# Key sums beside the value blocks, two last quotients in free banks, counts by column block, transfers in two parts and a layer norm in column chunks

## The chip, the core and the metric

The kernel runs on one core of one Trainium2 chip. Its engines run side by side and wait for one another through semaphores: TensorE (PE, with its weight loads PEld), VectorE (DVE), ScalarE (ACT), GpSimd (POOL) and SyncE (SP), which mostly issues transfers to the 16 DMA engines. The metric is the device time of one execution in microseconds; a few executions are timed and their median is compared. One execution is taken by the profiler.

## What is computed

A network of two layers on 1250 nodes of 768 features and 20000 edges. Cut to what matters here:

```
xn = layernorm(x)
x  = x + gcn(xn, edges) + linear_attention(xn)     # layer 0
x  = x + top2_of_8_experts(layernorm(x))
xn = layernorm(x)
x  = x + gat(gat(xn, 4 heads of 512), 1 head of 768) + flow_attention(xn)   # layer 1
x  = x + top2_of_16_experts(layernorm(x)) + shared_expert(layernorm(x))

layernorm(x) = (x - mean(x)) / sqrt(var(x) + 1e-5)
linear_attention: q, k = elu(.) + 1;  out = (q (k^T v)) / (q sum(k))   per head of 64
gat: e = leaky_relu(al_s[src] + al_d[dst]); softmax of e over the edges into a node; sum of h[src] by it
```

The edges are turned once into a dense matrix of counts (1250 by 1250); the graph parts multiply with it.

## The kernel before

The program is a list of stages, each a block in which every engine has its own code; a barrier ends each block. Nodes are laid out in two ways: node-major, ten tiles of 125 nodes on 125 partitions (`NT = 125`, `TILES = 10`), and feature-major, six tiles of 128 features on 128 partitions with 1254 columns, that is three chunks of `CW = 418` (`CH = 3`), which fill a bank of the 8-bank PSUM tensor `ps` each. Products that must be exact are made of three passes of rounded halves; others are plain float32 matmuls, which stand in the trace as two records each.

The stages that the change touches, in order of time:

- `norm_nodes_stage` loads the features x node-major in two transfers of five tiles (L139), takes statistics (L149), scales and transposes.
- `linear_attention_stage` makes keys and values for all ten tiles in `la_kv`, then for each of six blocks of 128 features (two heads) the product of keys and values (L258, ten tiles, bank p) and, into two more columns of the same bank, the product of the keys with a tile of ones (L261): the key sums. VectorE masks both into `kvb` and `denb`. Then q is projected, three chunks per block, and each of 18 units (block and chunk) gets a numerator (L270, bank 6) and a denominator (L271, bank 7); VectorE takes the reciprocal (L372) and multiplies (L374) before the next unit may write the two banks. TensorE runs four units behind the projection, so the last four follow it alone.
- `counts_stage` builds the counts row tile by row tile and stores for each a tile `far` (L437, 125 partitions, two buffers) that marks the absent edges; the stage ends when the last is stored (L439).
- `aggregate_stage` casts the counts to int16, tile by tile (L604), stores them to `counts_keep` (L617) and multiplies with them on TensorE (L673).
- `norm_stage`, three times (`ln1`, `ln2`, `ln3`): on feature-major x, TensorE averages all six tiles over 1254 columns (L806), VectorE subtracts (L818), ScalarE squares (L835), TensorE averages the squares (L811), then eps (L822), root (L837), reciprocal (L824) and scaling (L827), each over all 1254 columns.
- `graph_project_stage` projects to the four heads, tile by tile; ScalarE copies each result out of PSUM (L1946) and issues its store to `h_projected` itself (L1948, 40 of 250 KB). Far rows come in on SP (L1847).
- `graph_heads_stage`: per head and chunk the weights p of ten tiles are made (L2166, exponential, then times the counts in L2174), GpSimd sums them, TensorE aggregates the head's features with them (L2075). SP issues, in this order, the counts in three parts by tiles (L2051), the first head's features (L2043, 2500 KB on 125 partitions), the bias (L2053) and the second head's features.
- `graph_layer`, once, with one head: logits, then ten maxima over far rows (L2489, loaded by L2284 into two buffers), then weights and aggregation as above.

Transfers that SP issues go to its queue in the order of the code.

## Time and profile before

| | |
|---|---|
| median of 3 runs | 3528.55 us (3520.45 to 3528.65) |
| profiled execution, its own time | 3522.21 us |
| span of the profiled execution | 3520.4 us |
| PE busy | 2805.8 us (80%) |
| DVE busy | 1561.8 us (44%) |
| ACT busy | 829.2 us (24%) |
| moved by DMA | 314.17 MB, mean 89 GB/s |

The span is that of the profiled instructions; the execution's own time has what lies around it. Busy shares are means over stages with different limits, so what a stage waits for is read in that stage. PEclk in the windows is the granted TensorE clock, 1.00 for 2.4 GHz and 0.50 for 1.2 GHz.

### The profile page before, as it was taken

The page shows a single profiled execution, that of the slowest core. Times are in us where ns is not written, and L with a number is a line of the kernel's source. Part 1 is how long each engine was busy: PE and PEld are TensorE (multiplying, and loading weights), DVE is VectorE, ACT ScalarE, POOL GpSimd, SP SyncE. Part 2 cuts the span into 40 slices and gives each one's busy share as a digit, 9 for nine tenths or more (in the row PEclk, how much of TensorE's full clock was granted, in tenths as well). Part 3 has the DMA queues.
Part 4 walks back from the last instruction along what each step waited for, and adds up shares of the span by engine and source line. Part 5 has one row for each costly group of instructions (what it writes and reads, how often), then busy time and mean ns, then how long its engine had stood idle before and what let it go on. Part 6 is the DMA issues. An engine that isn't in the chain of part 4 may idle for free. (4 is left out here: it accounts for less than half of the span.)

```text
span 3520.4 us, 33065 instructions
## 1 busy us (share of the span) xinstructions
PE 2805.8 (80%) x12434; PEld 2168.8 (62%) x12434; DVE 1561.8 (44%) x2347; ACT 829.2 (24%) x1133; POOL 258.6 (7%) x251
## 2 busy tenths in 40 slices
PE   3997888897289767999999589995963966938884
PEld 3995454595289736857677445553962536727773
DVE  4327884413245434132345178872126433215554
ACT  2100012101145303201222234432102111025551
POOL 0000000000200100000000123320002100020002
PEclk9999999997589868979899799996985986969996
DMA  3500003200388512100223211104211001066664
GB/s 120 215 19 7 8 22 121 98 19 1 90 300 287 173 43 77 32 9 13 71 78 115 85 61 59 59 35 121 62 56 36 0 1 54 1 193 236 231 210 154
DMA packets 110470, 314.17 MB, mean 89 GB/s; under 512 B 40860, under 2 KB 50741, under 8 KB 101156
## 3 DMA queue, kind: packets, MB, share of 16 engines
q1 hardware_dynamic: 70572, 224.26, 18.4%
q10 hardware_dynamic: 21856, 57.43, 4.4%
q0 software_dynamic: 17920, 30.81, 3.3%
q8 instruction: 81, 1.33, 0.2%
q14 instruction: 41, 0.34, 0.0%
HBM read 215.33 MB, written 97.05 MB: 89 GB/s over the span
## 5 line engine op out<-in xcount | busy, mean ns | idle before, releaser
L2075 PE MATMUL ps<-g_p,g_h 125*128 125x418 f32 x960 | 341.9, 516 | 51.4 <-DMA g_h<-h_projected 51.4
L2075 PEld LDWEIGHTS ps<-g_p,g_h 125*128 125x128 f32 x960 | 182.8, 191 | 208.4 <-issue 156.5
L1097 PE MATMUL ps<-e_wh,e_xh 128*128 128x384 f32 (+1 forms) x600 | 220.6, 368 | 0.5 <-DVE e_wl L1316 0.5
L1097 PE MATMUL ps<-e_wh,e_xl 128*128 128x384 f32 (+1 forms) x600 | 214.1, 357 | 0.0
L1097 PE MATMUL ps<-e_wl,e_xh 128*128 128x384 f32 (+1 forms) x600 | 214.0, 357 | 0.0
L1326 DVE TENSOR_TENSOR e_xl<-ps,e_xh 128x768 fp32r<-128x768 f32 x68 | 65.1, 958 | 212.1 <-ACT e_xh L1267 212.1
L1097 PE MATMUL ps<-w_hi,h_hi 128*125 128x384 f32 x320 | 113.7, 355 | 43.2 <-DVE w_lo L2663 43.2
L1194 PE MATMUL ps<-ident,e_x 128*128 128x128 f32 x408 | 58.5, 282 | 111.1 <-DMA e_x<-expert_rows 111.1
L2351 PE MATMUL ps<-g_p,normed 125*128 125x418 f32 x360 | 130.1, 523 | 19.5 <-DVE g_p L2530 19.5
L2166 DVE SCALAR_TENSOR_TENSOR ps<-g_rows,g_logits,normed 125x418 f32<-125x418 f32 x120 | 126.8, 1066 | 34.0 <-DMA g_bias<-in_L_b 16.3
L548 PE MATMUL ps<-hot_src,hot_dst 125*125 125x418 f16 x588 | 125.8, 369 | 3.6 <-DVE hot_dst L492 3.6
L673 PE MATMUL ps<-counts,x 125*128 125x418 f32 x360 | 126.6, 513 | 0.0
L1316 DVE TENSOR_TENSOR e_wl<-e_w,e_wh 128x3072 fp32r<-128x3072 f32 (+1 forms) x34 | 101.4, 2982 | 46.2 <-ACT e_wh L1257 46.2
L2146 POOL TENSOR_TENSOR normed<-normed,g_p 125x418 f32<-125x418 f32 x108 | 109.7, 1016 | 133.7 <-DVE g_p L2174 130.3
L1097 PEld LDWEIGHTS ps<-e_wh,e_xl 128*128 128x128 f32 x600 | 113.6, 189 | 9.2
L1194 PEld LDWEIGHTS ps<-ident,e_x 128*128 128x128 f32 x408 | 49.0, 145 | 113.4 <-DMA e_x<-expert_rows 112.3
L1097 PEld LDWEIGHTS ps<-e_wh,e_xh 128*128 128x128 f32 x600 | 113.7, 190 | 8.1 <-issue 0.8
L1097 PEld LDWEIGHTS ps<-e_wl,e_xh 128*128 128x128 f32 x600 | 113.9, 190 | 7.6
L2351 PEld LDWEIGHTS ps<-g_p,normed 125*128 125x128 f32 x360 | 69.4, 193 | 79.4 <-issue 59.6
L491 DVE TENSOR_SCALAR hot_src<-index_row,edge_float 125x1254 f16<-125x1254 f16 x196 | 106.7, 544 | 25.5 <-PE ps L541 23.7
L1097 PE MATMUL ps<-attT_lo,la_hi 128*125 128x384 f32 x360 | 104.4, 345 | 12.4 <-DVE attT_lo L334 12.3
L1097 PE MATMUL ps<-w_lo,h_hi 128*125 128x384 f32 x320 | 111.7, 349 | 0.0
(433 smaller groups left out, 6058.9 us busy)
## 6 DMA issues: line engine op xcount, KB each, us to landing
e_w<-in_L_experts SPq DMA_DIRECT2D x32, 1152.0 KB, 6.2
e_w<-in_L_experts SPq DMA_DIRECT2D x18, 1536.0 KB, 7.1
e_x<-expert_rows SPq DMA_DIRECT2D x68, 384.0 KB, 5.1
expert_rows<-e_y ACTq DMA_DIRECT2D x68, 384.0 KB, 4.2
expert_rows<-la_zeros ACTq DMA_DIRECT2D x13, 1536.0 KB, 15.4
e_w<-in_L_experts SPq DMA_DIRECT2D x18, 768.0 KB, 5.1
h<-normed SPq DMA_DIRECT2D x48, 209.0 KB, 1.9
h_projected<-gp_h ACTq DMA_DIRECT2D x40, 250.0 KB
```

The costliest lines, as they stand in the source:

```text
L491: nc.vector.tensor_scalar(hs[:, u, :], idx[:], ef[:, 0, bass.ds(e, 1)], None, ALU.is_equal)
L548: mm = nc.tensor.matmul(ps[0:NT, b + c, 0:CW], hd[:, u, :], hs[:, u, cols(c)], start=False, stop=False, skip_group_check=True)
L673: mm = nc.tensor.matmul(ps[:, 3 * (f % 2) + c, 0:CW], k.x_node[:, t, P * f:P * f + P], k.counts[:, t, cols(c)], start=(t == 0), stop=(t == ...
L1097: mm = nc.tensor.matmul(out, lhs[a], rhs[b], start=(start and m == 0), stop=(stop and m == 2))
L1194: mm = nc.tensor.transpose(ps[:, f // 3, P * (f % 3):P * (f % 3) + P], x[:, b.x, P * f:P * f + P], k.ident[:])
L1316: nc.vector.tensor_tensor(wlo[:, b.w, 0:W1], w[:, b.w, 0:W1], whi[:, b.w, 0:W1].bitcast(F32), ALU.subtract)\
L1326: nc.vector.tensor_tensor(xlo[:, b.x, :, :].rearrange("p (b f) n -> p b (f n)", b=2), ps[:, 0:2, 0:3 * P], xhi[:, b.x, :, :].rearrange("p ...
L2075: mm = nc.tensor.matmul(ps[:, f, 0:CW], h_sb[:, i % 2, t, P * f:P * f + P], pr[:, n % 2, t, :], start=(t == 0), stop=(t == TILES - 1))
L2146: nc.gpsimd.tensor_tensor(sm[:, n % 2, :], sm[:, n % 2, :], pr[:, n % 2, t, :], ALU.add)\
L2166: nc.vector.scalar_tensor_tensor(out=t1(m), in0=rows[0:NT, i, 0, cols(c)], scalar=k.al[:, t, i:i + 1], in1=t2[:, m % 2, :], op0=ALU.add, o ...
L2351: mm = nc.tensor.matmul(ps[:, f, 0:CW], h_sb[:, i % HB, t, P * f:P * f + P], pr[:, n % 2, t, :], start=(t == 0), stop=(t == TILES - 1))
```

## The change

- *Key sums*: the value half of `la_kv` gets two columns of ones beside each block of 128 (`VW = 130`), set once by a memset; one product of 130 columns per tile and block gives values and sums. The 60 matmuls with the tile of ones are gone.
- *Last quotients*: `nd_bank` gives units 16 and 17 banks 0, 1 and 2, 3, which the projection no longer needs, and they no longer wait for the quotient before.
- *Counts by column block*: `counts_keep` and its copies are laid out by chunk (125 x 3 x 10 x 418). The head stage loads the first chunk, then the first head's features, then the other chunks; each chunk is waited for at its first use.
- *Transfers in two parts*: `two_parts` issues a transfer over 125 partitions as one of 112 and one of 13, each adding 16 to the semaphore; the waits ask for 32. It is used for the features, far rows (stores and both loads), counts (store and loads), the stores of `h_projected` and its loads.
- *Layer norm in chunks*: means, centring, squares, variances, roots and scaling run by chunk of 418 columns, in a staggered order, in `ln1`, `ln2` and `ln3`.

The diff, cut to its core:

```diff
+def two_parts(eng, dst, src, sem):
+
+    for part in (slice(0, 112), slice(112, NT)):
+        eng.dma_start(dst[part], src[part]).then_inc(sem, 16)
...
-                    sp.dma_start(k.x_node[:, 5 * g:5 * g + 5, :],
-                                 x_dram[625 * g:625 * g + 625, :].rearrange("(t p) d -> p t d", p=NT)).then_inc(loaded[g], 16)
+                    two_parts(sp, k.x_node[:, 5 * g:5 * g + 5, :],
+                              x_dram[625 * g:625 * g + 625, :].rearrange("(t p) d -> p t d", p=NT), loaded[g])
...
+        def nd_bank(v):
+
+            return 6 if v <= UNITS - CH else 2 * (v - UNITS + CH - 1)
...
-                        nc.tensor.matmul(ps[:, p, 0:P], kv[0:NT, t, P * p:P * p + P], kv[0:NT, t, D + P * p:D + P * p + P],
-                                         start=(t == 0), stop=(t == TILES - 1))
-                    for t in range(TILES):
-                        mm = nc.tensor.matmul(ps[:, p, P:P + 2], kv[0:NT, t, P * p:P * p + P], k.ones[0:NT, 0:2],
+                        mm = nc.tensor.matmul(ps[:, p, 0:VW], kv[0:NT, t, P * p:P * p + P], vb[:, t, p, :],
                                               start=(t == 0), stop=(t == TILES - 1))
...
-                    if v >= 1:
-                        pe.wait_ge(s["nd_out"], v)
-                    p, c = v // CH, v % CH
-                    nc.tensor.matmul(ps[:, 6, 0:CW], kvb[:, p, :], q[:, p % 2, cols(c)], start=True, stop=True)
-                    nc.tensor.matmul(ps[:, 7, 0:CW], denb[:, p, :], q[:, p % 2, cols(c)], start=True, stop=True)\
+                    if v <= UNITS - CH:
+                        if v >= 1:
+                            pe.wait_ge(s["nd_out"], v)
+                    p, c, b = v // CH, v % CH, nd_bank(v)
+                    nc.tensor.matmul(ps[:, b, 0:CW], kvb[:, p, :], q[:, p % 2, cols(c)], start=True, stop=True)
+                    nc.tensor.matmul(ps[:, b + 1, 0:CW], denb[:, p, :], q[:, p % 2, cols(c)], start=True, stop=True)\
...
+                nc.vector.memset(vb[:, :, :, P:VW], 1.0).then_inc(s["ones"], 1)
...
-                    nc.scalar.activation(whole[:, t, :], k.counts[:, t, :], ACT.Copy).then_inc(cast, 1)
+                    nc.scalar.activation(whole[:, :, t, :], k.counts[:, t, :].rearrange("p (c n) -> p c n", c=CH), ACT.Copy).then_inc(cast, 1)
...
-                sp.dma_start(k.counts_dram[:, :, :], whole[:]).then_inc(kept, 16)
+                two_parts(sp, k.counts_dram, whole[:], kept)
...
+                means(0)
+                means(1)
+                variances(0)
+                means(2)
+                variances(1)
+                variances(2)
...
+                def scale(c):
+                    dve.wait_ge(root, c + 1)
+                    nc.vector.reciprocal(r[:, c, :], r[:, c, :]).then_inc(rec, 1)
+                    dve.wait_ge(rec, c + 1)
+                    for f in range(FC):
+                        nc.vector.tensor_tensor(k.nT[:, f, cols(c)], k.nT[:, f, cols(c)], r[:, c, :], ALU.mult)
+                centre(0, range(FC))
+                centre(1, range(FC))
+                spread(0)
+                centre(2, range(FC))
+                scale(0)
+                spread(1)
+                spread(2)
+                scale(1)
+                scale(2)
...
+                squares(0)
+                squares(1)
+                roots(0)
+                squares(2)
+                roots(1)
+                roots(2)
...
-                        sp.dma_start(k.far_dram[t], far[:, t % 2, 0:T]).then_inc(far_out[t % 2], 16)
...
-                    act.dma_start(h_dram[n // TILES, :, n % TILES, :], h[:, n % HR, :]).then_inc(st[n % HR], 16)
+                    two_parts(act, h_dram[n // TILES, :, n % TILES, :], h[:, n % HR, :], st[n % HR])
...
-                    sp.dma_start(h_sb[:, i % 2], h_dram[i]).then_inc(h_in[i % 2], 16)
+                    two_parts(sp, h_sb[:, i % 2], h_dram[i], h_in[i % 2])
...
-                for q, (a, b) in enumerate(parts):
-                    sp.dma_start(counts[:, a:b, :], k.counts_dram[:, a:b, :]).then_inc(c_in[q], 16)
+                two_parts(sp, counts[:, 0], k.counts_dram[:, 0], c_in[0])
                 head_in(0)
+                for c in range(1, CH):
+                    two_parts(sp, counts[:, c], k.counts_dram[:, c], c_in[c])
...
-                        sp.dma_start(far[:, n % 2, :], k.far_dram[t]).then_inc(far_in[n % 2], 16)
+                        two_parts(sp, far[:, n % 2, :], k.far_dram[t], far_in[n % 2])
```

On SP, at the start of the graph heads, these transfers stood in the queue before (the counts, the features of the first head, the bias, the features of the second head):

```order
L2051 DMA g1_counts<-counts_keep 125x2508
L2051 DMA g1_counts<-counts_keep 125x5016 x2
L2043 DMA g1_h<-h1_projected 125x5120
L2053 DMA g1_bias<-in_L1_b1 128x16
L2043 DMA g1_h<-h1_projected 125x5120
```

And these stand there now, up to the second chunk of the counts; the third chunk, the bias and the second head follow:

```order
L98 DMA g1_counts<-counts_keep 112x4180
L98 DMA g1_counts<-counts_keep 13x4180
L98 DMA g1_h<-h1_projected 112x5120
L98 DMA g1_h<-h1_projected 13x5120
L98 DMA g1_counts<-counts_keep 112x4180
L98 DMA g1_counts<-counts_keep 13x4180
```

The first head's features moved ahead of two thirds of the counts, and ahead of the bias stand now eight issues instead of four.

On DVE, in the layer norm `ln1` (`normed` is the result, `ln_r` the root and its inverse), from the end of the projection before to the start of the router behind, this stood before:

```order
L787 SCALAR_TENSOR_TENSOR x<-ps,x_bias,x 128x1254 x2
L700 UNCONDITIONAL_BRANCH
L814 UNCONDITIONAL_BRANCH
L818 TENSOR_TENSOR normed<-x,ps 128x1254 x6
L822 TENSOR_SCALAR ln_r<-ps 128x1254
L824 RECIPROCAL ln_r<-ln_r 128x1254
L827 TENSOR_TENSOR normed<-normed,ln_r 128x1254 x6
L801 UNCONDITIONAL_BRANCH
```

And this stands there now:

```order
L841 TENSOR_TENSOR normed<-x,ps 128x418 x12
L845 TENSOR_SCALAR ln_r<-ps 128x418
L841 TENSOR_TENSOR normed<-x,ps 128x418 x6
L849 RECIPROCAL ln_r<-ln_r 128x418
L852 TENSOR_TENSOR normed<-normed,ln_r 128x418 x6
L845 TENSOR_SCALAR ln_r<-ps 128x418 x2
L849 RECIPROCAL ln_r<-ln_r 128x418
L852 TENSOR_TENSOR normed<-normed,ln_r 128x418 x6
```

The centring of the third chunk moved behind the first chunk's eps addition, and the first chunk's reciprocal and scaling ahead of the other two eps additions; the third chunk's reciprocal and scaling end the list.

## Rows read from the trace of the kernel before

**Rows 1.** The head of the page.

```profile
span 3520.4 us, 33065 instructions
```

**Rows 2.** Windows: length, busy time of PE, PEld, DVE, ACT, POOL, PEclk, DMA share, GB/s.

```profile
19.40:34.40 15.00, 0.00 (x0) 0.00 (x0) 4.70 (x10) 0.00 (x0) 0.00 (x0) 1.00 0.31 122
```

**Rows 3.** Timeline at the start: start us, duration us, engine, line, operation.

```profile
1.88 5.79 SPq L139 DMA_DIRECT2D x<-in_x  x2
34.46 4.70 DVE L149 BATCH_NORM_STATS2 ln_six<-x 125x6 f32<-125x384 f32 x10 [10.33 <-DMA x<-in_x]
```

**Rows 4.** DMA issues: tiles, queue, count, KB each, median us to landing.

```profile
x<-in_xT SPq DMA_DIRECT2D x1, 3750.0 KB, 13.6
fa_w<-in_L_v SPq DMA_DIRECT2D x6, 384.0 KB, 3.1
```

**Rows 5.** Timeline of the key and value products, first and last block.

```profile
196.60 2.39 PE L258 MATMUL ps<-la_kv 125*128 125x128 f32 x20
225.41 4.27 PE L261 MATMUL ps<-ones,la_kv 125*128 125x2 f32 x20
```

**Rows 6.** Windows, columns as in rows 2: the last block of sums.

```profile
226.00:230.00 4.00, 4.00 (x19) 4.00 (x19) 0.28 (x3) 0.00 (x0) 0.00 (x0) 0.50 0.00 0
```

**Rows 7.** Timeline of the last quotients.

```profile
339.20 2.77 DVE L372 RECIPROCAL la_kv<-ps 128x418 f32<-128x418 f32 x1 [3.31 <-PE ps L271]
342.74 1.69 PE L270 MATMUL ps<-la_kv,la_w 128*128 128x418 f32 x2 [3.58 <-DVE attT L374]
345.87 2.77 DVE L372 RECIPROCAL la_kv<-ps 128x418 f32<-128x418 f32 x1 [3.27 <-PE ps L271]
```

**Rows 8.** Timeline of the first layer norm of this form.

```profile
814.97 12.89 PE L806 MATMUL ps<-x,avg 128*128 128x418 f32 x36 [1.95 <-PEq L700]
830.70 14.61 PE L811 MATMUL ps<-ln_sq,avg 128*128 128x418 f32 x36 [2.84 <-ACT ln_sq L835]
848.12 7.99 DVE L824 RECIPROCAL ln_r<-ln_r 128x1254 f32<-128x1254 f32 x1 [1.31 <-ACT ln_r L837]
856.14 8.34 DVE L827 TENSOR_TENSOR normed<-normed,ln_r 128x1254 f32<-128x1254 f32 x6
```

**Rows 9.** Timeline: the second norm's means, the third one's variances.

```profile
1294.68 14.79 PE L806 MATMUL ps<-x,avg 128*128 128x418 f32 x36 [12.58 <-PEq L79]
2859.01 15.98 PE L811 MATMUL ps<-ln_sq,avg 128*128 128x418 f32 x36 [2.84 <-ACT ln_sq L835]
```

**Rows 10.** Groups by line: count, busy us, mean ns of one, idle before.

```profile
L374 DVE TENSOR_TENSOR attT<-ps,la_kv 128x418 f32<-128x418 f32 x18 | 10.7, 594 | 0.6
L835 ACT ACTIVATE ln_sq<-normed 128x1254 f32<-128x1254 f32 x18 | 22.5, 1249 | 261.3 <-DVE normed L818 246.2 <-PE ps L811 14.7
```

**Rows 11.** Waits of the SP queue: us in total, times, longest.

```profile
SPq L439 <- DMA far<-far_rows: 4.5, 1, 4.5
```

**Rows 12.** Timeline at the start of the graph heads.

```profile
1987.80 1.02 SPq L2051 DMA_DIRECT2D g_counts<-counts_keep  x3
1995.66 0.59 DVE L2174 SCALAR_TENSOR_TENSOR g_p<-ps,g_counts 125x418 f32<-125x418 f32 x1 [3.36 <-DMA g_counts<-counts_keep]
2007.03 0.58 DVE L2174 SCALAR_TENSOR_TENSOR g_p<-ps,g_counts 125x418 f32<-125x418 f32 x1
2009.13 0.58 DVE L2174 SCALAR_TENSOR_TENSOR g_p<-ps,g_counts 125x418 f32<-125x418 f32 x1
2034.19 9.77 PE L2075 MATMUL ps<-g_p,g_h 125*128 125x418 f32 x20 [51.44 <-DMA g_h<-h_projected]
```

**Rows 13.** Waits of the compute engines: us in total, times, longest.

```profile
ACT gp_h L1946 <- PE ps L1097: 99.8, 31, 7.2
DVE g_diag L2489 <- DMA g_far<-far: 15.1, 8, 3.2
```

**Rows 14.** Timeline of the maxima in the last graph layer.

```profile
2651.56 1.46 DVE L2489 CUSTOM_DVE_ANT_0 g_diag<-g_rows,g_far 125x1250 bf16<-125x1250 f32 x1 [3.16 <-DMA g_far<-far]
```

**Rows 15.** Timeline of ScalarE in the projection, its longest issue.

```profile
1865.64 1.19 ACTq L1948 DMA_DIRECT2D h_projected<-gp_h  x1
```

More of the change, by code:

```diff
@@ L254, in _ @@
                         mm.then_inc(s["kv_done"], 1)
+                pe.wait_ge(s["ones"], 1)
                 for p in range(FC):
@@ L814, in _, with variances @@
+                def variances(c):
+                    for f in range(FC):
+                        pe.wait_ge(sq, FC * c + f + 1)
+                        mm = nc.tensor.matmul(ps[:, 3 + c, 0:CW], k.avg[:], s[:, c % 2, f, :], start=(f == 0), stop=(f == FC - 1))
+                    mm.then_inc(var, 1)
+                means(0)
[4 more added lines that the diff above has]
+                variances(2)
             @block.vector
@@ L815, in _ @@
             def _(dve):
-                dve.wait_ge(mean, 1)
-                for f in range(FC):
-                    nc.vector.tensor_tensor(k.nT[:, f, :].rearrange("p (c n) -> p c n", c=CH),
-                                            k.xT[:, f, :].rearrange("p (c n) -> p c n", c=CH), ps[:, 0:CH, 0:CW],
-                                            ALU.subtract).then_inc(cen, 1)
-                dve.wait_ge(var, FC)
-                nc.vector.tensor_scalar(r3, ps[:, 3:6, 0:CW], EPS, None, ALU.add).then_inc(eps, 1)
@@ L823, in _, with centre @@
-                dve.wait_ge(root, 1)
-                nc.vector.reciprocal(r[:], r[:]).then_inc(rec, 1)
-                dve.wait_ge(rec, 1)
-                for f in range(FC):
-                    nc.vector.tensor_tensor(k.nT[:, f, :], k.nT[:, f, :], r[:], ALU.mult)
+                def centre(c, fs):
+                    if 0 in fs:
+                        dve.wait_ge(mean, c + 1)
+                    for f in fs:
+                        nc.vector.tensor_tensor(k.nT[:, f, cols(c)], k.xT[:, f, cols(c)], ps[:, c, 0:CW], ALU.subtract).then_inc(cen, 1)
@@ new lines, in spread @@
+                def spread(c):
+                    dve.wait_ge(var, c + 1)
+                    nc.vector.tensor_scalar(r[:, c, :], ps[:, 3 + c, 0:CW], EPS, None, ALU.add).then_inc(eps, 1)
+                def scale(c):
+                    dve.wait_ge(root, c + 1)
+                    nc.vector.reciprocal(r[:, c, :], r[:, c, :]).then_inc(rec, 1)
+                    dve.wait_ge(rec, c + 1)
+                    for f in range(FC):
+                        nc.vector.tensor_tensor(k.nT[:, f, cols(c)], k.nT[:, f, cols(c)], r[:, c, :], ALU.mult)
@@ L836, in _, with squares, roots @@
-                act.wait_ge(eps, 1)
-                nc.scalar.activation(r[:], r[:], ACT.Sqrt).then_inc(root, 1)
+                def squares(c):
+                    for f in range(FC):
+                        act.wait_ge(cen, FC * c + f + 1)
+                        if c >= 2:
+                            act.wait_ge(var, c - 1)
+                        nc.scalar.activation(s[:, c % 2, f, :], k.nT[:, f, cols(c)], ACT.Square).then_inc(sq, 1)
+                def roots(c):
+                    act.wait_ge(eps, c + 1)
+                    nc.scalar.activation(r[:, c, :], r[:, c, :], ACT.Sqrt).then_inc(root, 1)
```

78 lines of the change are left out of this document (35 added, 43 removed).

## The prediction

> **What bounds the kernel now.** I read the page's head first: the profiled execution has a span of 3520.4 us on its one core [rows 1], its own time is 3522.21 us, so 1.8 us lie around the span; the median of the three timed runs, 3528.55 us, is 6.3 us above it. The stages follow one another behind a barrier, so a microsecond that a stage ends earlier is a microsecond off the time, and the question for each edit is what ends its stage. I then read the waits, and the timeline at the places that the diff touches. Three kinds of place stand out there. First, transfers over 125 partitions: the second load of the node features keeps the 16 DMA engines busy at a mean share of 0.31, at 122 GB/s, with nothing but its own statistics beside it [rows 2], and the vector engine waits 10.33 us for it [rows 3]. 0.31 is 5 of 16. A load of twice the bytes over 128 partitions (3750 KB) lands in 13.6 us [rows 4], where the two of 125 partitions need 32.6 us, from the issue at 1.88 us to 34.46. Second, serial stretches: in the layer norm the tensor engine, then the vector engine, work alone one after the other [rows 8]; at the end of the linear attention the two take turns [rows 7]. Third, the key sums, on the tensor engine alone [rows 5].
>
> A rule of the Trainium skill ("DMA: Bandwidth & Descriptors", "Why a DMA increments its semaphore by 16 and not by 1") explains the share: a DMA runs on the largest number of engines up to 16 that divides its slowest dimension, so by it 125 rows use 5, 112 use 16 and 13 use 13. The trace agrees for 125 (0.31); no row here shows 112 or 13.
>
> **The change, part by part.** Everything is measured against 3522.2 us.
>
> *Feature loads.* Per engine 25 rows become at most 8. I take the 128-partition row of the same total: 13.6 us, plus about 1 us for two more issues, so the second half is there at 16.5 us instead of 34.46. The first half's statistics (4.70 us [rows 3]) fit in the wait for the second. Gain 18.0. Bounds: nothing if the limit is not the engines; 20.5 if 16 engines keep the 24.4 GB/s each that 5 had (122/5 [rows 2]).
>
> *Key sums.* Six value blocks at 2.39 us stand between 196.60 and 229.68 with the six blocks of sums; both were slower where the granted clock fell (0.50, that is 1.2 GHz, at 226 to 230) [rows 5, 6]. Afterwards 60 matmuls of 130 columns remain; at 130/128 of 2.39 us a block takes 2.43 and the stretch 14.6 instead of 33.1: gain 18.5. The tensor engine then keeps moving wide operands, so I expect the full clock (2.4 GHz) and add 1.5 us for the first projections behind it, which began at half clock. Bounds: if the clock stays at 1.2 GHz throughout, 29 us remain and 4 are gained; 20 at most. The extra memset of the ones stands on a vector engine that waits for the first cast anyway, 0.2 us if that cover is missing. The copies into the strided value blocks keep their size.
>
> *Last quotients.* The last two units wait for the vector engine (3.58 us before the tensor engine's last unit) and it for them (3.31 and 3.27) [rows 7]. With banks of their own, units 16 and 17 run beside the division of 15 and 16 (3.1 to 3.3 us, from 342.74 to 345.87, against 2.77 + 0.59 = 3.36 [rows 7, 10]), and the two idle gaps of the vector engine go: gain 6.6, bounds 5 and 6.7.
>
> *Layer norms, three times.* Before, the first runs from 814.97 to 864.48: means 12.89, then centring and the squares, variances from 830.70 to 845.31, then the root, one reciprocal of 7.99, scaling 8.34 [rows 8]. In pieces of 418 columns: a chunk's means or variances take a third of the 12.89 us, 4.2 to 4.3. A vector operation of 418 columns is spaced 0.51 us (ten of 384 take 4.70 [rows 3]; 0.47 x 418/384), a reciprocal of that size takes 2.77 [rows 7]. On the tensor engine stand means 0 and 1, variances 0, means 2: 16.9 us. The squares of chunk 0 are ready before the third of these begins at 8.5: centring follows the means at 4.3, ends at 7.4, and a square of three times the columns takes 1.25 [rows 10]. From there the vector engine sets the pace: centring 3.06, reciprocal 2.77, scaling 3.06, two eps additions 1.02, the wait for the root 0.1, then twice 2.77 + 3.06, and 0.1 to finish: 21.8. Together 38.7 against 49.5: gain 10.8. The second norm starts with 14.79 instead of 12.89 us, after an idle tensor engine, and keeps that: 10.7. The third lost 1.4 us (15.98 against 14.61) to the slow start of its variances after a gap [rows 9]; the gap goes: 12.2. Sum 33.7. Bounds: if the 0.594 us that one of 418 columns takes [rows 10] is also its spacing, 36 and 3 operations cost 3.3 us more per norm: 24; if part of the first gap on the vector engine is filled too, 37.
>
> *Counts by column block, loads of the head stage.* The stage begins at 1987.80; the column block needed first was in all three parts of the counts, and the first head's features were queued behind them. The products p of the first chunk wait for the counts (first at 1995.66), and the first aggregation for the features until 2034.19 [rows 12]. Afterwards 1020 KB of counts stand first: between 384 KB in 3.1 us and 3750 KB in 13.6, both over 128 partitions [rows 4], that is 5.1 us and an issue more, so first products near 1994. They follow at some 2.05 us each (2007.03 to 2009.13 [rows 12]), the last three closer, so the tenth is done near 2009. Counts block and features, 3.6 MB, are there at about 2002 by the 13.6 us of 3.84 MB; the bias, behind 5.7 MB, near 2008, so the vector engine's wait for it shrinks too. The products then set the start: 2009.2 instead of 2034.19, gain 25. Behind it the stage is paced by the tensor engine as before. Bounds 16 and 30.
>
> *Far rows in the last graph layer.* The maxima wait 15.1 us in eight waits [rows 13]. A maximum takes some 1.5 us; the one that starts at 2651.56 waited 3.16 us for its rows, whose buffer had come free when the maximum before last ended, so a row block comes 4.7 us after it may be asked for [rows 14]. A 384 KB load over 128 partitions lands in 3.1 us [rows 4]; with a second issue of about 0.4, 3.5. Two buffers give (1.5 + 3.5)/2 = 2.5 us per maximum; before it was 1.5 and a mean wait of 15.1/8 = 1.9, so 3.4: 8 x 0.9 = 7. The first of the eight may still wait longer; I take 6.5. Bounds 0 and 15.
>
> *Stores.* The counts stage ends with 4.5 us of waiting for the last far rows [rows 11]; by the same 3.5 us and a smaller block, gain 1.5. The projection's last store likewise 1. Its 40 stores become 80 issues on the scalar engine, at worst 1.19 us more each [rows 15]; that engine waits 99.8 us for the tensor engine there [rows 13], which covers even 40 x 1.19 = 48. If the cover were gone, those 48 would be the price. The counts store lies under the aggregation, which the tensor engine does without a wait for it, and gives nothing.
>
> Sum: 18.0 + 18.5 + 1.5 + 6.6 + 33.7 + 25 + 6.5 + 1.5 + 1 = 112.3; 3522.2 - 112.3 = **3410 us**.
>
> **The rivals.** *A: the splits give nothing*, because two parts on the same queue only follow one another. The Trainium skill says so ("DMA: Bandwidth & Descriptors", "Rules for kernel authors"): two transfers to disjoint partition halves are not worth it, since both halves already use all 16 engines. Against A stands the share of 0.31: before, eleven engines have nothing to do. In A remain 18.5 + 1.5 + 6.6 + 33.7 = 60.3, and in the head stage the order alone: 3.6 MB at 122 GB/s land near 2018, but the bias only near 2036, so about 10: 3522 - 70 = 3452 us. Chance 6%.
>
> *B: the staggered norm runs at the low clock*, as short waits on the squares let it drop (after the gap at 827.9 the first matmuls of variances were slow, so 14.61 us where 12.89 would do [rows 8]). The chain to the last centring is then 33.8 instead of 16.9, and each norm is 6 us longer than before: 33.7 + 18 lost, 3462 us. Against it: in the new order squares are ready before the tensor engine comes to them. Chance 5%.
>
> *C: slower than before*, by the doubled issues: the scalar engine carries 40 more in the projection. For the time to rise by 0.3% the extra issue would have to cost its cover of 99.8 us, the 112 us of gains and 11 more, 5.6 us each; the longest shown is 1.19. Then 3533 us or more. Chance 2%.
>
> *D: only the norms and transfers pay*, the clock in the key sums stays low and the maxima stay as they are: 14 + 1.5 + 6.5 less, 3432 us. Chance 12%. The forecast has the rest, 75%, with an own range of 3394 to 3426.
>
> **How the numbers follow.** Below 3394 lie all upper bounds together (20.5 + 20 + 1.5 + 6.7 + 37 + 30 + 15 + 3 + 2 = 136, 3386), which I don't expect at once. The range takes in D and stops short of A and B, which with C and the tails leave about 2 in 10 out: 3392 to 3442. A measurement of this kernel can tell about 0.3% (10.6 us) from no change. All cases but C end faster by more than that; a sum of small losses that I don't see gets 1%: faster 0.97, same 0.01, slower 0.02.
>
> **What would show it.** Feature loads: DMA share near 0.8 and statistics of the second half starting near 16.5 us. Key sums: no two-column matmuls, six blocks within 15 us at a granted clock of 1.00. Quotients: the last divisions back to back. Norms: 39, 41 and 39 us from the first mean to the last scaling, the vector engine idle only before centring. Heads: first aggregation 21 to 22 us after the stage begins, its waiter the products instead of the features. Last layer: maxima 2.3 to 2.5 us apart. The forecast is wrong if the share stays at 0.31, if the norms show a clock of 0.5, or if the head stage, starting earlier, waits later for products.

## The result, and the profile after

The changed kernel takes 3419.08 us (median of 4 runs, 3412.75 to 3424.46) where the kernel before took 3524.94 beside it (median of 4): a ratio of 0.970, with a 95% interval of 0.968 to 0.972. The forecast was 3410, from 3392 to 3442. The profiled execution has a span of 3417.5 us; before it was 3520.4 [rows 1].

Start of the kernel after, from its timeline and its windows (columns as in rows 2 and 3):

```profile
1.89 2.16 SPq L98 DMA_DIRECT2D x<-in_x  x4
12.81 4.70 DVE L155 BATCH_NORM_STATS2 ln_six<-x 125x6 f32<-125x384 f32 x10 [10.78 <-DMA x<-in_x]
20.47 4.69 DVE L155 BATCH_NORM_STATS2 ln_six<-x 125x6 f32<-125x384 f32 x10 [2.96 <-DMA x<-in_x]
...
4.00:19.00 15.00, 0.00 (x0) 0.00 (x0) 4.70 (x10) 0.00 (x0) 0.00 (x0) 1.00 0.99 248
```

The second half of the features is there at 20.47 us instead of 34.46 [rows 3]. The engines' share is 0.99 instead of 0.31 [rows 2], but three times the engines move only twice the bytes: 248 GB/s, that is 15.7 GB/s each where five moved some 25 each. 248 is a mean, too. With all engines busy, the rate swings inside the window:

```profile
6.00:8.00 2.00, 0.00 (x0) 0.00 (x0) 0.00 (x0) 0.00 (x0) 0.00 (x0) 1.00 1.03 286
10.00:12.00 2.00, 0.00 (x0) 0.00 (x0) 0.00 (x0) 0.00 (x0) 0.00 (x0) 1.00 1.05 128
```

The low stretch lies just before the first half's landing lets the statistics begin at 12.81 us; which rows move in it, the trace doesn't show.

Key sums and last quotients after, from the timeline, and a window inside the key sums:

```profile
183.05 13.56 PE L271 MATMUL ps<-la_kv 125*128 125x130 f32 x120
196.37 0.44 PE L1140 MATMUL ps<-la_hi,la_w_parts 128*128 128x418 f32 x1
...
185.00:195.00 10.00, 10.00 (x92) 10.00 (x91) 3.77 (x17) 0.84 (x1) 0.00 (x0) 1.00 0.26 80
...
294.37 1.73 PE L281 MATMUL ps<-la_kv,la_w 128*128 128x418 f32 x2 [3.58 <-DVE attT L388]
297.53 2.77 DVE L386 RECIPROCAL la_kv<-ps 128x418 f32<-128x418 f32 x1 [3.31 <-PE ps L282]
300.85 2.76 DVE L386 RECIPROCAL la_kv<-ps 128x418 f32<-128x418 f32 x1
304.15 2.76 DVE L386 RECIPROCAL la_kv<-ps 128x418 f32<-128x418 f32 x1
```

The six blocks take 13.6 us at the full granted clock, where 33.1 were needed (196.60 to 229.68 [rows 5]); the last two divisions follow without a wait, where each of the last two waited 3.3 us [rows 7]. The one before them, at 297.53, still waits 3.31 us, as in the kernel before.

The first norm after, from the timeline (it ends at 808.90 + 3.11):

```profile
773.12 8.66 PE L820 MATMUL ps<-x,avg 128*128 128x418 f32 x24 [1.95 <-PEq L714]
777.60 3.09 DVE L841 TENSOR_TENSOR normed<-x,ps 128x418 f32<-128x418 f32 x6 [4.88 <-PE ps L820]
...
790.24 3.09 DVE L841 TENSOR_TENSOR normed<-x,ps 128x418 f32<-128x418 f32 x6 [3.62 <-PE ps L820]
793.25 2.76 DVE L849 RECIPROCAL ln_r<-ln_r 128x418 f32<-128x418 f32 x1
...
808.90 3.11 DVE L852 TENSOR_TENSOR normed<-normed,ln_r 128x418 f32<-128x418 f32 x6
```

From 773.12 to 812.01 it takes 38.9 us, before 49.5 [rows 8]. What is left is the vector engine's idle 3.62 us ahead of the third centring, and the chain behind it. The second norm takes 40.5 (51.3 before), the third 40.6 (50.9), more than the first, since their first 24 matmuls take 10.3 us instead of 8.66 (row below for the third).

Start of the graph heads after, from the timeline, and then the start of the third norm:

```profile
1917.08 0.75 SPq L98 DMA_DIRECT2D g_counts<-counts_keep  x2
1923.95 0.59 DVE L2216 SCALAR_TENSOR_TENSOR g_p<-ps,g_counts 125x418 f32<-125x418 f32 x1 [2.37 <-DMA g_counts<-counts_keep]
1939.41 9.04 PE L2118 MATMUL ps<-g_p,g_h 125*128 125x418 f32 x20 [25.78 <-DVE g_p L2216]
...
2740.95 10.35 PE L820 MATMUL ps<-x,avg 128*128 128x418 f32 x24 [2.37 <-PEq L2313]
```

The first aggregation comes 22.3 us after the stage's start (46.4 before), and it now waits for the products g_p, no longer for a transfer [rows 12].

Waits of the kernel after, those of the projection (first row) and of the last graph layer:

```profile
ACT gp_h L1989 <- PE ps L1140: 109.3, 37, 3.6
DVE g_diag L2531 <- DMA g_far<-far: 7.1, 6, 1.8
DVE g_diag L2513 <- DMA g_a<-in_L_att: 12.3, 1, 12.3
PE ps L2393 <- DVE g_p L2572: 19.5, 1, 19.5
```

The same two places before, where the forecast showed no row of it, with rows from the middle of the projection:

```profile
ACT gp_h L1946 <- DMA h_projected<-gp_h: 16.0, 5, 4.3
DVE g_rows L1982 <- DMA g_rows<-far: 8.3, 3, 3.7
DVE g_diag L2471 <- DMA g_a<-in_L_att: 9.4, 1, 9.4
...
1885.22 3.36 DVE L1959 TENSOR_TENSOR gp_w_lo<-gp_w,gp_w_hi 128x3072 fp32r<-128x3072 f32 x1
1888.64 0.50 PE L1097 MATMUL ps<-gp_w_hi,normed_hi 128*125 128x512 f32 x1 [1.86 <-DVE gp_w_lo L1959]
...
1880.00:1920.00 40.00, 38.14 (x163) 29.81 (x162) 25.99 (x35) 10.35 (x13) 0.00 (x0) 0.96 0.35 117
```

The maxima wait 7.1 us for their far rows instead of 15.1 [rows 13]. Three rows stand out that the forecast did not have. In the projection the scalar engine had waited 16.0 us for its own stores, before it could read the next bank, and the vector engine 8.3 us for far rows; both waits are gone. And in the last layer the vector engine waits longer than before, 12.3 instead of 9.4 us, for the attention rows g_a, whose loads the change does not touch.

By stage, in us gained, from the first and last instructions of the stages in both profiles (for the projection and the feature loads up to the start of the next stage; the start of the graph heads is read from the length of the whole stage):

```
term                                    forecast  measured
feature loads                             18.0      13.0
key sums                                  18.5      19.5
first projections, last quotients          8.1       9.2
end of the counts stage                    1.5       0.6
norms, first / second / third   10.8 10.7 12.2   10.6 10.8 10.3
projection                                 1         5.3
start of the graph heads                  25        24.8
last graph layer                           6.5       6.7
sum                                      112.3     110.8
third norm's end to the end of the run     0        -9.7
other stages                               0         1.8
span                                     112.3     102.9
```

### The profile page after: what moved, and what is told of

It is laid out like the page before. It is cut to its first block and busy times, and to the rows that moved or that the text cites. A ratio compares the mean times of both kernels' runs of the same rounds, so it can differ in the third digit from the quotient of the medians.

```text
span 3417.5 us, 33039 instructions
## 1 busy us (share of the span) xinstructions
PE 2779.7 (81%) x12314; PEld 2152.4 (63%) x12314; DVE 1567.5 (46%) x2432; ACT 835.8 (24%) x1175; POOL 259.5 (8%) x251
## 5 line engine op out<-in xcount | busy, mean ns | idle before, releaser
L2393 PE MATMUL ps<-g_p,normed 125*128 125x418 f32 x360 | 129.4, 521 | 19.5 <-DVE g_p L2572 19.5
L1140 PE MATMUL ps<-attT_lo,la_hi 128*125 128x384 f32 x360 | 104.0, 344 | 12.5 <-DVE attT_lo L345 12.3
```

The costliest lines, as they stand in the source:

```text
L1140: mm = nc.tensor.matmul(out, lhs[a], rhs[b], start=(start and m == 0), stop=(stop and m == 2))
L2393: mm = nc.tensor.matmul(ps[:, f, 0:CW], h_sb[:, i % HB, t, P * f:P * f + P], pr[:, n % 2, t, :], start=(t == 0), stop=(t == TILES - 1))
```

## The experiments

All kernels are the changed kernel with the edit shown, unless said otherwise. Times are medians, and places are read from the profiles. The experiments ran on several chips; each ratio is against the kernel before on the same chip.

**1. Two parts, but by columns.** `two_parts` cuts each transfer across its columns:

```diff
-    for part in (slice(0, 112), slice(112, NT)):
-        eng.dma_start(dst[part], src[part]).then_inc(sem, 16)
+    cut = dst.shape[1] // 2
+    for part in (slice(0, cut), slice(cut, dst.shape[1])):
+        eng.dma_start(dst[:, part], src[:, part]).then_inc(sem, 16)
```

> Every split transfer of the changed kernel is cut in two again, but across its columns: both parts keep all 125 partitions, number of issues and bytes stay. If the split pays because 125 partitions use 5 engines and 112 use 16, the gain of the splits goes: feature statistics of the second half near 34 us instead of 20.5 (+13), projection +5, far rows of the last graph layer +5, head stage waits for its features again (+12, the order kept): about 3454 us, DMA share of the loads near 0.31. If any two parts beside each other do it (for instance on two different groups of five engines), the share is 0.6 or more and the time 3419 to 3428 us. If the splits give nothing at all, as in rival A, 3419 us.

Measured 3459.58 us, ratio 0.981 (0.979 to 0.984). Window over the loads, and the heads' wait:

```profile
4.00:33.00 29.00, 0.00 (x0) 0.00 (x0) 4.70 (x10) 0.00 (x0) 0.00 (x0) 1.00 0.32 126
...
PE ps L2119 <- DMA g_h<-h_projected: 35.8, 1, 35.8
```

The share is that of before, and the statistics of the second half begin at 34.80 us. Two transfers beside each other on the same rows give nothing; what pays is that the rows divide otherwise. That is the first case, 3454 us. By it some 40 us of the 106 belong to the splits.

**2, 3, 4. Other partitions: 100 and 25, 119 and 6, 64 and 61.** The number 112 is changed, here to 100, and to 119 and to 64 in the other two:

```diff
-    for part in (slice(0, 112), slice(112, NT)):
+    for part in (slice(0, 100), slice(100, NT)):
```

> The parts are 100 and 25 partitions instead of 112 and 13. If a transfer uses the largest divisor up to 16, 100 rows use 10 engines and 25 use 5, so the busiest engine has 15 rows instead of 8. If the feature load of the changed kernel (233 GB/s, share 0.96) is limited by something that all engines share, 10 engines at 24.4 GB/s each reach the same rate: second half's statistics near 21 us, time within 4 us of 3419. If each engine moves only the 14.6 GB/s that it showed there, 15 rows of 30.7 KB take 32 us: statistics near 34 us and a time near 3440 us.

> The parts are 119 and 6 partitions: by the largest divisor 7 engines with 17 rows each, and 6 engines with one more. Five engines moved 24.4 GB/s each, ten and sixteen some 15. If an engine keeps its 24 GB/s while few others work, 18 rows of 30.7 KB take 22.6 us: statistics of the second half near 25 us, share 0.44 at about 170 GB/s. If the lower rate belongs to a split in two transfers and not to the number of engines, 18 rows at 14.8 GB/s take 37 us: near 40 us, later than before the change.

> The parts are nearly equal, 64 and 61 partitions. If only the balance of two halves counts, 3419 us and statistics near 20.5 us. If the largest divisor up to 16 counts, 64 rows use 16 engines and 61, a prime number, one engine: 61 rows of 30.7 KB at 24.4 GB/s take 77 us, statistics of the second half near 79 us (+58), first aggregation of the head stage some 70 us after its start (+48): 3525 us or more, slower than before the change.

Measured 3444.81 us, ratio 0.978 (0.975 to 0.981), for 100 and 25; a single run each gave 3461.13 for 119 and 6, and 3838.13 for 64 and 61. Windows over the loads of the three, in this order, the third while its 64 rows and then while its 61 rows run:

```profile
4.00:19.00 15.00, 0.00 (x0) 0.00 (x0) 0.00 (x0) 0.00 (x0) 0.00 (x0) 1.00 0.65 165
```

```profile
4.00:19.00 15.00, 0.00 (x0) 0.00 (x0) 0.00 (x0) 0.00 (x0) 0.00 (x0) 1.00 0.45 132
```

```profile
5.00:8.00 3.00, 0.00 (x0) 0.00 (x0) 0.00 (x0) 0.00 (x0) 0.00 (x0) 1.00 1.03 200
12.00:34.00 22.00, 0.00 (x0) 0.00 (x0) 0.00 (x0) 0.00 (x0) 0.00 (x0) 1.00 0.06 25
```

The shares are those of the divisors: 0.65 of 16 is 10 engines, 0.45 is 7, and while the 61 rows run one engine of sixteen is busy (0.06), at 25 GB/s. 64 and 61, nearly equal halves, are 310 us slower than the kernel before: the second half's statistics begin at 88.18 us, the heads' features are waited for 98.9 us, and the projection's stores for 134.7. But the rate of an engine is not what I had taken it for. Five moved 25 GB/s each, seven 18 (132 / 7.2), ten 16, and sixteen on 64 partitions 12. So with 100 and 25 the second of the two cases came (statistics of the second half at 32.64 us); with 119 and 6 neither did (33.76 us, between 25 and 40); with 64 and 61 only the direction was foreseen, 3525 us or more.

**5. The norm of before** in the changed kernel (the function as it was).

> The changed kernel with the norm stage of before. By the traces the three norms took 49.5, 51.3 and 50.9 us before and 38.9, 40.5 and 40.6 after: +31.7, so about 3451 us, and everything else as in the changed kernel. Rival: the 6 to 10 us that the changed kernel lost in its second expert stage come with the new norm (it ends that stage's start at another point of the clock's course): then only +22 to +26, about 3443 us, and the second expert stage as short as before.

Measured 3451.51 us, ratio 0.979 (0.977 to 0.982), 32 us over the changed kernel. That is the 31.7 us that the traces give, so the rival of 22 to 26 us did not come. Its first norm:

```profile
774.89 12.88 PE L820 MATMUL ps<-x,avg 128*128 128x418 f32 x36 [1.95 <-PEq L714]
790.61 14.61 PE L825 MATMUL ps<-ln_sq,avg 128*128 128x418 f32 x36 [2.83 <-ACT ln_sq L849]
```

These are the durations of rows 8 to 0.01 us. From the third norm's start to the end of the run this kernel takes 680.2 us, 669.9 without the 10.3 that its norm is longer. The changed kernel took 676.6 there, the kernel before 666.8 (677.1 less 10.3). The other kernels of this section, whose code behind the third norm is the same, show 670.7 to 674.6, and experiment 12 665.2 (with the 3.2 added where the norm is shorter). So the 9.7 us lost there don't hang on the norm: experiment 12 has a shorter norm still and none of the loss. The same code differs by up to 11 us from one profile to the next, and the two profiles compared here lie near the ends. For the kernel before, one profile is all there is; whether it is usually shorter there stays open.

**6. The old order of the head stage.** Counts in three parts by tiles, ahead of the features, each part still split:

```diff
-                two_parts(sp, counts[:, 0], k.counts_dram[:, 0], c_in[0])
+                for q, (a, b) in enumerate(((0, 2), (2, 6), (6, TILES))):
+                    two_parts(sp, counts[:, :, a:b], k.counts_dram[:, :, a:b], c_in[q])
                 head_in(0)
-                for c in range(1, CH):
-                    two_parts(sp, counts[:, c], k.counts_dram[:, c], c_in[c])
...
```

> The changed kernel with the counts of the head stage loaded in three parts by tiles (0 to 1, 2 to 5, 6 to 9) ahead of the first head's features, each part still split at 112 partitions. If the split transfers carry most of the head stage's gain, 5.7 MB at 233 GB/s land some 26 us after the stage's start, and the products are ready at 22: first aggregation near 26.5 instead of 22.3, +4 us, about 3423 us. If the order carries it (10 us, as in rival A of the forecast, or more), 3429 us or more. If the products set the start whatever the order, 3419 us.

Measured 3427.96 us, ratio 0.972 (0.970 to 0.974): the interval holds the changed kernel's 0.970, so the place must tell. The tensor engine waits there for the features again:

```profile
PE ps L2117 <- DMA g_h<-h_projected: 33.3, 1, 33.3
```

The first aggregation comes 29.9 us after the stage's start, 3.4 us later than this case's estimate, against 22.3 in the changed kernel and 46.4 before. In experiment 1, which has the new order and no split over partitions, it comes at 30.8. From the projection's last copy to the first aggregation, the end of the last store included, pass 32.7 us here, 35.2 in experiment 1, 25.1 in the changed kernel and 50.8 before.

But the start is not the stage. From its first to its last instruction the stage takes 397.2 us before, 389.8 with the order alone (experiment 1), 381.0 with the splits alone (here) and 372.4 with both. The order alone gains 7.4, the splits alone 16.1, both 24.8, so the two nearly add up. In experiment 1 a part of the earlier start is lost again behind it, at the second chunk:

```profile
1984.17 1.23 DVE L2210 SCALAR_TENSOR_TENSOR ps<-g_rows,g_logits,normed 125x418 f32<-125x418 f32 x2 [21.24 <-DMA g_bias<-in_L_b]
2004.77 7.71 PE L2119 MATMUL ps<-g_p,g_h 125*128 125x418 f32 x15 [6.04 <-DVE g_p L2217]
```

By the profile, the vector engine waits there for the bias, which stands behind counts and features in the queue, and the tensor engine then for the vector engine's products.

**7. Separate key sums.** The matmul of 130 columns becomes one of 128, and ten of two columns follow each block:

```diff
-                        mm = nc.tensor.matmul(ps[:, p, 0:VW], kv[0:NT, t, P * p:P * p + P], vb[:, t, p, :],
+                        nc.tensor.matmul(ps[:, p, 0:P], kv[0:NT, t, P * p:P * p + P], vb[:, t, p, 0:P],
...
+                        mm = nc.tensor.matmul(ps[:, p, P:VW], kv[0:NT, t, P * p:P * p + P], k.ones[0:NT, 0:2],
```

> The changed kernel, but each of the six value blocks is again ten matmuls of 128 columns and then ten of 2 columns for the key sums; all the rest stays. If the key sums' stretch was long for its 120 matmuls, half of them narrow, and for the clock that fell during the narrow ones, it returns from 13.3 us to about 33, with granted clocks of 0.5 to 0.8 in parts of it, and the first projections behind it begin at the lower level: +21 us, about 3440. If the clock fell for another reason (its place in the run), the six blocks take 6 x (2.39 + 2.29) = 28 us at the full clock: +15, about 3434.

Measured 3445.04 us, ratio 0.975 (0.972 to 0.979). Two blocks of the timeline, and two windows with PEclk:

```profile
182.88 2.39 PE L271 MATMUL ps<-la_kv 125*128 125x128 f32 x20
213.46 4.27 PE L274 MATMUL ps<-ones,la_kv 125*128 125x2 f32 x20
...
188.00:193.00 5.00, 5.00 (x47) 5.00 (x46) 0.55 (x3) 0.84 (x1) 0.00 (x0) 1.00 0.01 3
198.00:203.00 5.00, 5.00 (x26) 5.00 (x25) 0.00 (x0) 0.00 (x0) 0.00 (x0) 0.50 0.24 79
```

The stretch is 34.9 us long (182.88 to 217.73), +21.3 over 13.6. The first three blocks still run at the full clock; then the granted clock falls to 0.50, the level of 1.2 GHz, while the tensor engine is busy without a gap. The changed kernel kept 1.00 at the same place, so the clock did not fall for its place in the run; it fell in a stretch of 128-column and 2-column matmuls that lasts longer. Whether the narrow columns did it or the length of the stretch, no run tells: here, too, its first 13 us ran at 1.00.

**8. Attention rows first.** In the last graph layer the sync engine waits for them before it issues the rest:

```diff
+                    sp.wait_ge(at_in, 32)
                 far_rows(0, range(2))
```

> In the last graph layer the sync engine waits until the two attention rows have landed before it issues the far rows and the counts. In the changed kernel the vector engine waited 12.30 us for these two loads, 9.35 before, with the same issues ahead of them. If the split transfers behind them slowed them (they now use all 16 engines beside them), the wait is 9.4 us or less and the first maximum comes 3 us sooner. If the loads had another reason to be late (where the stage happens to start), 12.3 stays. The whole time can't show 3 us in one look.

A single run took 3424.92 us. The wait:

```profile
DVE g_diag L2514 <- DMA g_a<-in_L_att: 9.7, 1, 9.7
```

9.7 us instead of 12.3, as before the change (9.4). In experiment 1 it is 9.9, with 100 and 25 partitions 11.0, in the other kernels with 112 and 13 that leave these loads as they are it is 12.2 to 13.0. The split transfers behind the two loads slow them: a cost of the change of some 3 us.

**9. A norm without the gap** at the third centring:

```diff
-                def scale(c):
+                def invert(c):
                     dve.wait_ge(root, c + 1)
                     nc.vector.reciprocal(r[:, c, :], r[:, c, :]).then_inc(rec, 1)
+
+                def scale(c, fs):
                     dve.wait_ge(rec, c + 1)
...
                 spread(0)
+                invert(0)
                 centre(2, range(FC))
-                scale(0)
-                spread(1)
+                scale(0, range(3))
+                spread(1)
+                scale(0, range(3, FC))
+                invert(1)
                 spread(2)
-                scale(1)
-                scale(2)
+                scale(1, range(FC))
+                invert(2)
+                scale(2, range(FC))
```

> In the changed norm the vector engine idles 3.6 us before the third centring while the first chunk's variances are ready. Here the reciprocal of the first chunk goes into that gap, and the eps addition of the second stands in the middle of the first scaling. By the spacings of the changed kernel each norm takes 36.1 instead of 38.9 us: -2.8, three times -8.4: about 3411 us. Rival: the clock or the scalar engine's roots (they stand ahead of the last squares) delay the third chunk's variances: 0 to -3 in all, 3416 to 3419 us.

Measured 3409.64 us, ratio 0.967 (0.964 to 0.969). The first norm runs from 770.13 to 805.84, 35.7 us; the second and third take 37.4 each. That is 3.1 to 3.2 less than in the changed kernel, three times; 2.8 was expected.

**10. Four edits together**, the norm of experiment 9 among them:

```diff
+    pieces = ((0, 4), (4, 7), (7, 9), (9, 10))
...
-                for g in range(2):
...
+                for g, (a, b) in enumerate(pieces):
...
+                        for lo, hi in ((0, 112), (112, NT)):
+                            sp.dma_start(a_rows[lo:hi, j, :], att_dram[j, 0].partition_broadcast(hi - lo)).then_inc(at_in, 16)
+                    sp.wait_ge(at_in, 64)
...
+                            if n == 0 and f == 0:
+                                pe.wait_ge(s["p_made"], t + 1)
```

> Four edits on the changed kernel: the norm order of the run before this one (-8.4); the feature load in pieces of 4, 3, 2 and 1 tiles, so that only one tile's statistics follow the last landing (-3); the attention rows of the last graph layer loaded in two parts and ahead of the far rows (wait 12.3 becomes some 5.5: -7); the first aggregation of the head stage and of the last layer waits for its products one by one, so that nine of its first ten matmuls lie beside the products (-4 in each; the sum on another engine, due 2.4 us after the last product, holds it back). Sum -26: about 3393 us. If the second half of these are eaten by a lower clock of an engine that starts and stops (the aggregations) and by slower landings of more pieces, -13: about 3406 us.

Measured 3391.08 us, ratio 0.962 (0.959 to 0.964). The statistics end at 21.78 us instead of 25.16, and the waits of the last layer, with the start of the heads' aggregation, are:

```profile
DVE g_diag L2528 <- DMA g_a<-in_L_att: 5.5, 1, 5.5
PE ps L2408 <- DVE g_p L2587: 7.3, 5, 5.1
...
1927.93 9.79 PE L2128 MATMUL ps<-g_p,g_h 125*128 125x418 f32 x20 [21.04 <-DMA g_h<-h_projected]
```

The attention rows are waited for 5.5 us, and the first aggregation there waits 7.3 us, in five pieces, for its products, where it waited 19.5 at once. The heads' second aggregation starts 4 us earlier after the stage's start than in the changed kernel (27.9 instead of 31.9), but the first waits for the features again.

**11. The first head's features in two halves by tiles**, on experiment 10:

```diff
+                    if i == 0:
+                        two_parts(sp, h_sb[:, 0, 0:5], h_dram[0][:, 0:5], h_half)
+                        two_parts(sp, h_sb[:, 0, 5:TILES], h_dram[0][:, 5:TILES], h_in[0])
+                        return
                     two_parts(sp, h_sb[:, i % 2], h_dram[i], h_in[i % 2])
...
```

> The best kernel so far with one edit: the first head's features arrive in two halves by tiles (0 to 4, 5 to 9). In the best kernel the first aggregation waited for the features until 21 us after the stage's start, and its first ten matmuls then took 9.8 us at the lower clock. If the features alone hold it back, five of the ten run while the second half lands: -4 to -5 us, about 3386. If the products or the sum on the other engine hold it back right behind, 0 to -1: 3390.

Measured 3395.17 us, ratio 0.962 (0.960 to 0.963): no gain. The aggregation starts at 11.7 us and then waits for the products; its second starts 25.1 us after the stage's start, 2.8 earlier than in experiment 10, and in the whole time nothing of it is left to be seen.

**12. Feature tiles over 128 partitions**, on experiment 10 (x_wide is the same buffer with all its partitions):

```diff
-                for g, (a, b) in enumerate(pieces):
-                    two_parts(sp, k.x_node[:, a:b, :],
-                              x_dram[NT * a:NT * b, :].rearrange("(t p) d -> p t d", p=NT), loaded[g])
+                for t in range(TILES - 1):
+                    sp.dma_start(k.x_wide[:, t, :], x_dram[NT * t:NT * t + P, :]).then_inc(loaded[t // 3], 16)
+                two_parts(sp, k.x_node[0:NT, TILES - 1, :], x_dram[NT * (TILES - 1):T, :], loaded[3])
...
```

> The best kernel (e8) with one edit: each of the first nine feature tiles is loaded with 128 rows to 128 partitions (three rows of the next tile lie unused in the last three partitions), the tenth as before in 112 and 13. 64 rows on 16 engines ran at some 200 GB/s, 112 and 13 at 233, while a load over 128 partitions before the change went at 401 to 421 GB/s with all engines busy too. If the place of the partitions sets the rate, as in the Trainium skill's port rule (SBUF - State Buffer, Door 1: The DMA port swizzle), the nine tiles run near 400 GB/s, three tiles are there some 6.5 us after the start, the statistics follow without a gap and end near 16.5 instead of 21.8 us: -5, about 3386 us. If the source (rows of 3072 bytes) or sixteen busy engines as such hold it at 233 GB/s, the statistics end near 20.5: -1, about 3390 us.

Measured 3383.55 us, ratio 0.960 (0.958 to 0.962), the lowest median of all. The interval overlaps that of experiment 10 (0.959 to 0.964), so the gain is read from its place. The first and last statistics of the timeline, and windows:

```profile
8.31 5.79 DVE L155 BATCH_NORM_STATS2 ln_six<-x 125x6 f32<-125x384 f32 x12 [6.27 <-DMA x<-in_x]
14.93 3.78 DVE L155 BATCH_NORM_STATS2 ln_six<-x 125x6 f32<-125x384 f32 x8 [0.83 <-DMA x<-in_x]
...
4.00:14.00 10.00, 0.00 (x0) 0.00 (x0) 5.62 (x12) 0.00 (x0) 0.00 (x0) 1.00 0.99 357
10.00:12.00 2.00, 0.00 (x0) 0.00 (x0) 1.93 (x5) 0.00 (x0) 0.00 (x0) 1.00 1.02 412
```

The same bytes from the same rows of 3072 bytes, with all engines as busy as in the changed kernel, come at 357 GB/s over ten microseconds and at 412 at best, and the statistics end at 18.71 us, 3.1 earlier than in experiment 10 (I had expected 16.5: the first three tiles came at 8.3, not 6.5). So neither the source nor sixteen busy engines as such held the changed kernel at 248 GB/s. What points to the partitions that a transfer covers is this run together with the 64 rows of experiment 4, which ran at 200 GB/s in transfers of five tiles like the changed kernel's. Here the loads are of one tile each; whether that has a share in the gain was not tested.

## Why the forecast was right, and where its terms were off

The mechanism of each edit that the forecast costed was as foreseen, and the result lies in the likeliest case's own range. That the sum of the terms is only 1.5 us off is in part luck: feature loads (-5.0), the third norm (-1.9) and the counts stage (-0.9) are balanced by the projection (+4.3), the linear attention (+2.1) and less.

Rival A, that splits give nothing, is refuted by experiment 1, where without them the kernel takes 40 us more; and by experiment 4 parts pay only where their rows divide among more engines. The rule that it drew on, that two transfers to disjoint partition halves are not worth it (the Trainium skill, "DMA: Bandwidth & Descriptors", "Rules for kernel authors"), takes for granted that both halves use all 16 engines, and 125 rows don't. The same page's rule on the largest divisor ("Why a DMA increments its semaphore by 16 and not by 1") holds in every share seen: 0.32 for 125, 0.45 for 119, 0.65 for 100, 0.99 for 112 and 13.

Rival B (a low clock in the new norm) came only at the start of the second and third norm, where the first 24 matmuls take 1.6 to 1.7 us more than in the first; the second norm had such a start before, too (14.79 against 12.89 us [rows 8, 9]). Rival C did not come: the scalar engine waits 109.3 us for the tensor engine in the projection, more than before, so the doubled issues are covered. Of rival D, the clock in the key sums did not stay low, and the maxima did move.

**Feature loads, 18.0 forecast, 13.0 measured.** The step that was mis-sized is "I take the 128-partition row of the same total". 112 partitions are not 128. (The statistics in the window of rows 2 are the first half's and not those of the load beside them; no term hangs on that.) The second half's statistics begin at 20.47 us instead of 16.5, which is 4.0 of the 5.0; the last 1.0 is lost behind them, since the stage takes that much longer from there, and its cause is not shown. The rate per engine fell from 25 to 15.7 GB/s, and experiment 12 shows that over 128 partitions it doesn't (412 GB/s at a share of 1.02 are 25 each). The Trainium skill ("SBUF — State Buffer", "Door 1: The DMA port swizzle") says that a transfer's rate depends on how many of 16 ports its partitions reach, that 64 partitions reach 8 of them, and gives 218 GB/s as their limit and 436 for 128; the traces agree with 200 for 64 (experiment 4) and 412 for 128. That engines of the 112-row part stand at one port at the same time fits the rates between, but is only argued: no run measured a port.

**Projection, 1 forecast, 5.3 measured.** From the last copy to the next stage's first issue pass 2.8 us instead of 4.4, so the last store gave 1.6. The other 3.7 came from a transfer that I did not cost here: the far rows, which this stage loads too, over 125 partitions. Before, the vector engine waited 8.3 us for them in three waits. Behind its maxima stands, on the same engine, the low part of the next head's weights (L1959), and the tensor engine idled 1.86 us for it. With the slower clock behind that (0.96 on the mean of the 40 us above, by my estimate 1.6 us) this makes 3.5 of the 3.7. In the changed kernel the wait for far rows is gone, and the same low part begins 93.4 us after the stage's start instead of 101.1. The scalar engine's 16.0 us of waiting for its own stores looks larger, but the tensor engine's matmuls never wait for that engine in this stage, and no run shows that it was worth anything.

**Last graph layer, 6.5 forecast, 6.7 measured, by errors that cancel.** The series of ten maxima is 7.9 us shorter (29.9 to 22.0), more than I gave it; the attention rows come 2.9 us later, which I had not seen at all, though I had asked elsewhere what a faster transfer would collide with. A further 1.7 us is gained behind the maxima, where no cause was looked for.

**Third norm, 12.2 forecast, 10.3 measured.** The slow start of the variances went, as forecast, but the first means start slowly instead (10.35 us for 24 matmuls, 8.66 in the first norm).

**Heads, 25 forecast, 24.8 measured:** place, size and waiter as forecast. Rival A gave the order alone 10 of it, because the bias would come late; in the stage's length it is 7.4, and experiment 1 shows that wait for the bias.

The forecast of 3410 lies 9 us below the median. The terms account for 1.5 of that; the rest is the last stretch, which took 9.7 us longer in the profile of after, without any edit in it, less 1.8 us that other stages gained. What sets it in one execution or another stays open.

## What to carry to other kernels

Read the share of the DMA engines in the window of a transfer that something waits for, not its rate alone: 0.31 was five engines of sixteen, and the partition count set it. Splitting 125 rows into 112 and 13 doubles the rate; loading 128 rows, the three spare ones unused, brings it to three times that of before. A transfer that becomes faster can delay one ahead of it that stayed narrow (12.3 us of waiting instead of 9.7, experiment 8): after such a change look at every load issued just before. And an earlier start is not yet a shorter stage: compare both.

## What the runs showed of the hardware that I had not expected

With all 16 DMA engines busy, the same 3072-byte rows moved at 200 GB/s to 64 partitions, 248 to 112 and 13, and 357 to 412 to 128. With equal numbers of issues, nearly equal halves (64 and 61) cost 419 us against 112 and 13, in a single run. And a tensor engine that was busy without a gap, with blocks of 128-column and of 2-column matmuls in turn, was granted 0.50 of its clock in parts of the last 21 of 35 us, while 60 matmuls of 130 columns in their place took 13.6 us and kept 1.00.
